# Who issues the loads of the key sums, and when the sums are made, in an attention kernel on one core

## The chip, the cores and the metric

One Trainium2 chip, one of its cores. The metric is the device time of one execution in microseconds. TensorE is called PE, VectorE DVE, ScalarE ACT, GpSimd POOL and SyncE SP in the profile.

## The reference

Cross attention with 16 heads of 64: 1024 queries, 6404 keys, model width 128, all float32, then a projection, a residual and a normalization.

```python
Q = (input_Q @ W_Q).reshape(b, -1, 16, 64).transpose(0, 2, 1, 3)      # x: (1, 1024, 128)
K = (input_K @ W_K).reshape(b, -1, 16, 64).transpose(0, 2, 1, 3)      # context: (1, 6404, 128)
V = (input_V @ W_V).reshape(b, -1, 16, 64).transpose(0, 2, 1, 3)
attn = softmax(einsum('bhqd,bhkd->bhqk', Q, K) / sqrt(64), axis=-1)
context = einsum('bhqk,bhkd->bhqd', attn, V).transpose(0, 2, 1, 3).reshape(b, -1, 1024)
out = context @ W_O + input_Q
return (out - mean(out)) / sqrt(var(out) + 1e-5)
```

## The kernel before

The heads go in eight pairs (0 to 7), and a pair in two halves of the queries (h = 0, 1), which makes 16 passes t. A pass runs over 50 chunks c of 128 keys; u counts the chunks of all passes. In step u PE computes the scores of chunk u + 2 (line 661) and adds the product of the probabilities and the values of chunk u (line 678). ACT makes the exponential of the scores (line 975, into a ring of four), DVE adds up the probabilities (line 1114). Each wait between engines is a semaphore; every engine runs its own list of instructions in the order in which it is written, and so does the DMA queue of the engine that issues a transfer.

Between the steps PE also computes the keys and values of the pair in blocks of four chunks; `work_at(t, c)` says which piece stands at which chunk. There are 12 full blocks and a rest. In pairs 1 to 7 the keys of the full blocks are computed by a Strassen-like scheme with seven products instead of eight. It needs sums of pieces of the context (the key sums, `c_forms`, here "forms", 384 KB per block) and of the weights. In a pass with h = 0 block b = c // 4 + 2 is served: at c % 4 = 0 the first round ("r", `seven_first`, lines 758 to 765), behind the product of its step, then three copies by ACT (`cross`, lines 991 and 993) and two sums by POOL (`sum_crossed`, lines 614 and 617); at c % 4 = 2 the second round ("k", `seven_second`, lines 776 to 780), which DVE takes out of PSUM (`take_seven`, lines 1095 to 1100); at c % 4 = 3 the values ("v", line 727), taken at line 1071. Blocks 0 and 1 of the next pair are served in the pass with h = 1, at chunks 38 to 45. The two rounds and the values share one pair of PSUM banks, so each waits until the one before is taken out.

The forms are the same for all pairs. POOL makes them once, in the first pass, from the context and a copy of it with its halves swapped (`form_keys`, four operations per block, lines 580 to 589, one after the other as their data comes). SP stores each block to DRAM (`store_forms`). From then on SP loads them, block by block and pair by pair, into the two places of `c_forms` (`load_forms`, line 460), 84 loads in all. A load waits for the second round that used the place before it, two blocks earlier. Where these loads stand among SP's other transfers is written out by hand in the loop of lines 478 to 510. That loop also carries the sums of the last pass: DVE folds them at chunk 8 of the next pass (line 1168), four small copies turn them (line 485), DVE inverts them at chunk 12 (lines 1176 to 1183), and they go through DRAM to all partitions (lines 491 to 501), for POOL's normalization at chunk 17. In a pass with h = 0 the loads of blocks 2 to 4 stand ahead of the wait for the fold, those of blocks 5 and 6 behind the four small copies, and the others behind the transfers of the inverses.

ACT issues two loads at the start (lines 995 and 996) and none after.

The loop of ACT, in short:

```python
for u in range(UNITS):
    t, c = place(u)
    if u + AHEAD < UNITS:
        exps(u + AHEAD)
    found = work_at(t, c)
    if found is not None and found[0] == "r":
        cross(found[1], found[2])
```

Of the kernel before, what the change touches and what calls it, by code (L numbers as in the profile page):

```python
# [6 lines left out]
ALU = mybir.AluOpType  # L7
# [4 lines left out]
def cross_attention_kernel(nc: bass.Bass, xT: bass.AP, x: bass.AP, ctxT: bass.AP, w_q: bass.AP,  # L12
# [27 lines left out]
    PAIRS = HD // (2 * DH)  # L40
    SCALE = float(DH) ** -0.5
    P = 128
# [19 lines left out]
    FULL_BLOCKS = NK // BK  # L62
# [18 lines left out]
    NORM_STEP, W_FORMS_STEP = 17, 24  # L81
    LAST_BLOCK_STEPS = (42, 45)
    LEFT_BEHIND = 7
    FORM_COLS = 2 * 3 * P
    assert NQH == 2 and BLOCKS == 13 and TAIL_CHUNKS == 3 and QT == 8
    assert CHUNKS == FULL_CHUNKS + 1 and LEFT_ROWS == DH

# [3 lines left out]
    def place(u):  # L91

        t = min(u // FULL_CHUNKS, PASSES - 1)
        return t, u - t * FULL_CHUNKS

    def by_seven(pair, b):

        return pair > 0 and 0 <= b < FULL_BLOCKS

    def seven_index(pair, b):  # L100
        return (pair - 1) * FULL_BLOCKS + b
# [34 lines left out]
    COUNT, READY = {}, {}  # L136
# [7 lines left out]
    with ctx:  # L144
# [53 lines left out]
        c_forms = sb("c_forms", [P, 2, FORM_COLS])  # L198
# [208 lines left out]
        def _(sp):  # L407
# [42 lines left out]
                sp.wait_ge(c_forms_ready, b + 1)  # L450
                sp.dma_start(forms_dram[b, :, :], c_forms[:, b % 2, :]).then_inc(c_forms_stored[b % 2], 16)

            def load_forms(pair, b):
                n = seven_index(pair, b)
                if n < 2:
                    for slot in range(2):
                        sp.wait_ge(c_forms_stored[slot], 16 * (FULL_BLOCKS // 2))
                else:
                    sp.wait_ge(work_done, COUNT["k", pair - (b < 2), (b - 2) % FULL_BLOCKS])
                sp.dma_start(c_forms[:, n % 2, :], forms_dram[b, :, :]).then_inc(c_forms_loaded[n % 2], 16)  # L460

            def load_turned_w(pair):
                if pair > 1:
# [13 lines left out]
            sp.wait_ge(left_zeroed, 2)  # L477
            for t in range(PASSES - 1):
                pair, h = (t + 1) // 2, (t + 1) % 2
                if h == 0:  # L480
                    for b in range(2, 5):
                        load_forms(pair, b)
                sp.wait_ge(quad_sums_ready, t + 1)
                for i in range(QUADS):
                    sp.dma_start(quad_rows[:, i, :], quad_sums[i * SQ:(i + 1) * SQ, :]).then_inc(quad_rows_loaded, 16)  # L485

                if h == 0:
                    for b in range(5, 7):
                        load_forms(pair, b)
                sp.wait_ge(inv_lines_ready, t + 1)  # L490
                sp.dma_start(inv_dram[t, :].rearrange("(j a) -> j a", a=SQ), inv_lines[:, :]).then_inc(inv_written, 16)
                sp.wait_ge(inv_written, 16 * (t + 1))
                if t > 0:
                    sp.wait_ge(norm_done, t)
                for head in range(2):
                    sp.dma_start(inv_sum[part(head), :], inv_dram[t, head * QH:(head + 1) * QH]
                                 .partition_broadcast(DH)).then_inc(inv_loaded, 16)
                for head in range(2):
                    row = t % 2 * DH + (t // 2 * 2 + head) * LEFT
                    sp.dma_start(inv_left[row:row + LEFT, :], inv_dram[t, head * QH:(head + 1) * QH]  # L500
                                 .partition_broadcast(LEFT)).then_inc(inv_left_loaded, 16)
                if t + 1 < PASSES - 1:
                    load_left(t + 1)
                if h == 1 and pair + 1 < PAIRS:
                    load_turned_w(pair + 1)
                    for b in range(2):
                        load_forms(pair + 1, b)
                if h == 0:
                    for b in range(7, FULL_BLOCKS):
                        load_forms(pair, b)  # L510

            def general():
                def load_weights(pair):
# [32 lines left out]
        def _(pool):  # L546
# [19 lines left out]
                nc.gpsimd.tensor_tensor(out=attn[:, pair, h * QH:(h + 1) * QH], in0=o_b[:, :], in1=inv_sum[:, :],  # L566
                                        op=ALU.mult).then_inc(norm_done, 1)

            def form_keys(b):

                one, two = part(b % 2), part(1 - b % 2)
                as_is = ctx_all[:, b * BK:(b + 1) * BK].rearrange("p (i e k) -> p i e k", i=2, e=2)
                turned = turned_ctx(b).rearrange("p (i e k) -> p i e k", i=2, e=2)
                forms = c_forms[:, b % 2, :].rearrange("p (i f k) -> p i f k", i=2, f=3)
                pool.wait_ge(ctx_loaded[b], 16)
                pool.wait_ge(chunk_loaded, 16)
                pool.wait_ge(turned_ctx_loaded[b % 2], 48 * (b // 2 + 1))
                if b > 0:
                    pool.wait_ge(c_forms_ready, b)
                nc.gpsimd.tensor_tensor(out=forms[one, :, 0:2, :], in0=as_is[one, :, :, :], in1=turned[one, :, :, :],  # L580
                                        op=ALU.add).then_inc(c_form_step, 1)
                pool.wait_ge(c_form_step, 3 * b + 1)
                nc.gpsimd.tensor_tensor(out=forms[two, :, 0, :], in0=as_is[two, :, 1, :], in1=turned[two, :, 0, :],
                                        op=ALU.subtract).then_inc(c_form_step, 1)
                pool.wait_ge(c_form_step, 3 * b + 2)
                nc.gpsimd.tensor_tensor(out=forms[two, :, 1, :], in0=as_is[two, :, 0, :], in1=as_is[two, :, 1, :],
                                        op=ALU.add).then_inc(c_form_step, 1)
                pool.wait_ge(c_form_step, 3 * b + 3)
                nc.gpsimd.tensor_tensor(out=forms[two, :, 2, :], in0=turned[two, :, 0, :], in1=turned[two, :, 1, :],
                                        op=ALU.add).then_inc(c_forms_ready, 1)  # L590

            def form_weights(pair):

# [25 lines left out]

            pool.wait_ge(identity_ready, 2)  # L620
            pool.wait_ge(left_zeroed, 2)
            for b in range(FULL_BLOCKS):
                form_keys(b)
            pool.wait_ge(c_forms_ready, FULL_BLOCKS)
            for t in range(1, PASSES):
                for c in range(FULL_CHUNKS):
# [341 lines left out]
        def _(act):  # L968
# [14 lines left out]
            def cross(pair, b):  # L983
# [8 lines left out]
                                         ACT.Copy).then_inc(crossed_ready, 1)  # L992
                nc.scalar.activation(crossed[:, 0, :], seven_slots(b)[2], ACT.Copy).then_inc(crossed_ready, 1)  # L993

            act.dma_start(wq_sb[:, 0:2 * DH], w_q[:, 0:2 * DH]).then_inc(first_w_loaded["q"], 16)
            act.dma_start(xT_sb[:, 0:QH], xT[:, 0:QH]).then_inc(x_loaded[0], 16)
            for found in WHOLE:
# [3 lines left out]
# [4 lines that stand above are left out]
                found = work_at(t, c)  # L1005
                if found is not None and found[0] == "r":
                    cross(found[1], found[2])
                if t == 0 and c == LEFT_EXP_STEP:

                    act.wait_ge(work_ready, READY["sl", 0, 0])  # L1010
                    nc.scalar.activation(p_left[:, :], p_left[:, :], ACT.Exp, scale=SCALE).then_inc(left_ready, 1)
                if c == chunks_of(t) - 1:

                    act.wait_ge(pv_done, u + 1)
                    if t > 0:

                        act.wait_ge(norm_done, t)
                    nc.scalar.activation(o_a[:, :], o_ps[:, 0, :], ACT.Copy).then_inc(o_a_ready, 1)  # L1018
# [359 lines left out]
```

## Time and profile before

| | |
|---|---|
| median of 3 runs | 1603.39 us (1603.27 to 1603.54) |
| profiled execution | 1603.11 us, span 1601.3 us |
| granted clock of TensorE, mean | 0.999 |
| PE busy | 1586.4 us, 99% |
| DVE, ACT, POOL busy | 84%, 58%, 18% |
| DMA, mean over the span | 35 GB/s |

The busy time of PE contains modelled ends: a matmul counts as busy until its modelled end, also when the next one has already started. Idle time of PE in the profile is therefore what is left after these ends; the distance between the starts of two groups shows more.

### The profile page before, as it was taken

Reading aid. Unit: us, or ns where it says so; the run is one execution under the profiler, and the core shown is the slowest. Engines: PE = TensorE matmul, PEld = TensorE weight load, DVE = VectorE, ACT = ScalarE, POOL = GpSimd, SP = SyncE. Lnnn points to the kernel's source line nnn. Section 1 sums busy time; section 2 is a strip of 40 time slices with the busy share of each in tenths; the row PEclk is TensorE's granted clock in tenths of the full one; section 3 lists DMA queues with packets and bytes.
Section 4 is the critical chain, followed back from the end, with each engine's and each line's share of the span. In section 5 each row is a group of like instructions: output and inputs, shape, how many; then the busy total and the mean of one; then the engine's idle time right before and its main releaser. Section 6 shows DMA issues by size and latency. Waiting matters only on the chain.

```text
span 1601.3 us, 43898 instructions
## 1 busy us (share of the span) xinstructions
PE 1586.4 (99%) x19164; PEld 1028.4 (64%) x19164; DVE 1346.4 (84%) x1397; ACT 929.7 (58%) x1080; POOL 294.5 (18%) x313
## 2 busy tenths in 40 slices
PE   9999999999999999999999999999999999999998
PEld 4576666666666666666666666666666666666435
DVE  7898798887988878887798878888788887898877
ACT  4345566556555556656566566565666555656653
POOL 4842012120121201202022021120111102111000
PEclk9999999999999999999999999999999999999999
DMA  6320002010110001100011000110011100110000
GB/s 214 94 76 31 11 22 69 12 31 11 42 58 2 30 22 39 51 2 31 21 49 41 2 31 21 59 32 2 30 32 49 32 2 30 32 59 22 9 1 15
DMA packets 31618, 56.68 MB, mean 35 GB/s; under 512 B 7120, under 2 KB 13392, under 8 KB 31424
## 3 DMA queue, kind: packets, MB, share of 16 engines
q1 hardware_dynamic: 31136, 53.51, 10.6%
q8 instruction: 153, 2.51, 0.7%
q14 instruction: 41, 0.34, 0.1%
q10 hardware_dynamic: 288, 0.33, 0.1%
HBM read 48.02 MB, written 5.30 MB: 33 GB/s over the span
## 4 chain that ended last, share of the span: by engine, by line
PE 93%; DVE 3%; DMA 2%; issue 1%; SPq 1%; ACT 0%; DVEq 0%; ACTq 0%
PE s_ps L661 41%; PE o_ps L678 41%; PE w_ps L727 5%; PE w_ps L744 2%; DMA c_forms<-forms_dram 2%; DVE sums L1114 1%; SPq L485 1%; PE w_ps L758 1%; PE w_ps L763 1%; PE w_ps L780 1%; DVE quad_sums L1168 1%; PE w_ps L779 1%; PE w_ps L759 0%; PE w_ps L776 0%; PE w_ps L765 0%
## 5 line engine op out<-in xcount | busy, mean ns | idle before, releaser
L975 ACT ACTIVATE probs<-s_ps 128x1024 f32<-128x1024 f32 x801 | 820.6, 1025 | 619.2 <-PE s_ps L661 611.7
L1114 DVE TENSOR_TENSOR sums<-sums,probs 128x1024 f32<-128x1024 f32 x785 | 986.3, 1256 | 123.1 <-ACT probs L975 89.8
L678 PE MATMUL o_ps<-probs,v_all 64*64 64x512 f32 x6408 | 927.2, 589 | 0.0
L661 PE MATMUL s_ps<-q_sb,k_all 64*64 64x512 f32 x6408 | 924.7, 589 | 0.0
L678 PEld LDWEIGHTS o_ps<-probs,v_all 64*64 64x64 f32 x6408 | 412.4, 133 | 219.1 <-issue 89.3
L661 PEld LDWEIGHTS s_ps<-q_sb,k_all 64*64 64x64 f32 x6408 | 401.2, 133 | 202.0 <-issue 76.7
L614 POOL TENSOR_TENSOR crossed<-crossed 128x128 f32<-128x128 f32 x84 | 43.6, 519 | 721.3 <-ACT crossed L993 721.3
L1071 DVE TENSOR_REDUCE v_all<-w_ps 128x512 f32<-128x1024 f32 (+2 forms) x103 | 122.0, 1184 | 41.8 <-PE w_ps L727 41.6
L727 PEld LDWEIGHTS w_ps<-wv_sb,ctx_all 64*64 64x64 f32 x3176 | 110.4, 133 | 42.6 <-issue 16.6
L727 PE MATMUL w_ps<-wv_sb,ctx_all 64*64 64x128 f32 x3176 | 117.3, 269 | 0.0
L991 ACT ACTIVATE crossed<-w_ps 64x384 f32<-64x384 f32 x168 | 81.6, 486 | 24.2 <-PE w_ps L765 22.0
L617 POOL TENSOR_TENSOR crossed<-crossed 128x128 f32<-128x128 f32 x84 | 90.6, 1078 | 6.6
L560 POOL TENSOR_TENSOR o_b<-o_a,o_b 128x512 f32<-128x512 f32 x15 | 23.5, 1565 | 248.8 <-ACT o_a L1018 248.8
L1095 DVE TENSOR_TENSOR k_all<-crossed,w_ps 128x256 f32<-128x256 f32 x84 | 35.3, 420 | 37.3 <-POOL crossed L617 27.2
L566 POOL TENSOR_TENSOR attn<-o_b,inv_sum 128x512 f32<-128x512 f32 x15 | 25.8, 1718 | 210.9 <-DMA inv_sum<-inv_dram 210.9
L780 PEld LDWEIGHTS w_ps<-ctx_all,w_forms 64*64 64x64 f32 x336 | 41.3, 133 | 25.9 <-issue 18.5
L1097 DVE TENSOR_REDUCE k_all<-w_ps 128x256 f32<-128x512 f32 x84 | 57.4, 683 | 0.0
L758 PEld LDWEIGHTS w_ps<-c_forms,w_forms 64*64 64x64 f32 x336 | 21.2, 131 | 49.0 <-DVE v_all L1071 39.4
L780 PE MATMUL w_ps<-ctx_all,w_forms 64*64 64x128 f32 x336 | 51.3, 269 | 0.0
L779 PE MATMUL w_ps<-c_forms,w_forms 64*64 64x128 f32 x336 | 48.9, 269 | 0.0
L779 PEld LDWEIGHTS w_ps<-c_forms,w_forms 64*64 64x64 f32 x336 | 39.3, 133 | 4.3 <-issue 3.2
L758 PE MATMUL w_ps<-c_forms,w_forms 64*64 64x128 f32 x336 | 34.6, 274 | 5.8 <-DMA c_forms<-forms_dram 5.8
(115 smaller groups left out, 686.1 us busy)
## 6 DMA issues: line engine op xcount, KB each, us to landing
c_forms<-forms_dram SPq DMA_DIRECT2D x84, 384.0 KB, 3.1
forms_dram<-c_forms SPq DMA_DIRECT2D x12, 384.0 KB, 2.6
inv_sum<-inv_dram SPq DMA_DIRECT2D x30, 128.0 KB, 2.8
attn<-in_ctxT SPq DMA_DIRECT2D x24, 128.0 KB, 3.3
ctx_all<-in_ctxT SPq DMA_DIRECT2D x11, 256.0 KB, 5.3
quad_rows<-quad_sums SPq DMA_DIRECT2D x60, 4.0 KB, 1.8
c_forms<-in_ctxT SPq DMA_DIRECT2D x12, 64.0 KB, 2.4
x_sb<-in_x SPq DMA_DIRECT2D x1, 512.0 KB, 10.1
```

The lines of the kernel that those rows point to most:

```text
L617: nc.gpsimd.tensor_tensor(out=crossed[:, 0, :], in0=crossed[:, m3, :], in1=crossed[:, m1, :], op=ALU.subtract).then_inc(crossed_summed, 1)
L661: last = nc.tensor.matmul(s_ps[part(half), u % 2, head * QH:(head + 1) * QH], k_all[part(head), c * P + half * DH:c * P + (half + 1) * DH] ...
L678: last = nc.tensor.matmul(o_ps[part(head), rows, :], v_all[part(rows), key_chunk(t, c, head), part(head)], probs[part(rows), u % RING, hea ...
L727: last = nc.tensor.matmul(banks[rows][part(half), m * P:(m + 1) * P], ctx_all[part(rows), at_key:at_key + DH], wv_sb[part(rows), at * P:(a ...
L758: nc.tensor.matmul(main[g, 0, 1, :], w_form(one, 0, 1 - i), form(one, pair, b, i, 0), start=True, stop=True)
L779: nc.tensor.matmul(main[part(i), 1, 0, :], w_form(one, 1, i), form(one, pair, b, i, 2), start=True, stop=True)
L780: last = nc.tensor.matmul(main[part(1 - i), 0, 0, :], w_form(one, 2, 1 - i), ctx_all[part(one), at:at + P], start=True, stop=True)
L975: nc.scalar.activation(probs[:, u % RING, :], s_ps[:, u % 2, :], ACT.Exp, scale=SCALE).then_inc(probs_ready, 1)
L991: nc.scalar.activation(crossed[part(1 - half), 1:4, :], apart[part(half), :, :], ACT.Copy).then_inc(crossed_ready, 1)
L1071: return nc.vector.tensor_reduce(out=target, in_=banks.rearrange("p r n -> p n r"), axis=AX.X, op=ALU.add)
L1097: nc.vector.tensor_reduce(out=target[:, :, 1, :], in_=main.rearrange("p j s k -> p j k s"), axis=AX.X, op=ALU.add)
L1114: nc.vector.tensor_tensor(out=sums[0:rows, t % 2, :], in0=sums[0:rows, t % 2, :], in1=probs[0:rows, u % RING, :], op=ALU.add).then_inc(sum ...
```

## The change

The loads of the forms leave SP's list, but for the first two (pair 1, blocks 0 and 1). ACT gets them: in its loop, in the step after a second round, and behind the exponential of that step, it waits for that second round and issues the load of the block two further on, which may belong to the next pair. POOL makes the forms in steps: operation number n of the 48 (n = 0 to 47) waits, beside what it waited for, until exponential number n is done. Nothing that is computed changes.

```diff
--- before.py
+++ after.py
@@ -81,7 +81,7 @@
     NORM_STEP, W_FORMS_STEP = 17, 24
     LAST_BLOCK_STEPS = (42, 45)
     LEFT_BEHIND = 7
-    FORM_COLS = 2 * 3 * P
+    FORM_COLS, FORM_STEPS = 2 * 3 * P, 4
     assert NQH == 2 and BLOCKS == 13 and TAIL_CHUNKS == 3 and QT == 8
     assert CHUNKS == FULL_CHUNKS + 1 and LEFT_ROWS == DH
 
@@ -450,14 +450,11 @@
                 sp.wait_ge(c_forms_ready, b + 1)
                 sp.dma_start(forms_dram[b, :, :], c_forms[:, b % 2, :]).then_inc(c_forms_stored[b % 2], 16)
 
-            def load_forms(pair, b):
-                n = seven_index(pair, b)
-                if n < 2:
-                    for slot in range(2):
-                        sp.wait_ge(c_forms_stored[slot], 16 * (FULL_BLOCKS // 2))
-                else:
-                    sp.wait_ge(work_done, COUNT["k", pair - (b < 2), (b - 2) % FULL_BLOCKS])
-                sp.dma_start(c_forms[:, n % 2, :], forms_dram[b, :, :]).then_inc(c_forms_loaded[n % 2], 16)
+            def load_first_forms():
+                for slot in range(2):
+                    sp.wait_ge(c_forms_stored[slot], 16 * (FULL_BLOCKS // 2))
+                for b in range(2):
+                    sp.dma_start(c_forms[:, b, :], forms_dram[b, :, :]).then_inc(c_forms_loaded[b], 16)
 
             def load_turned_w(pair):
                 if pair > 1:
@@ -477,16 +474,10 @@
             sp.wait_ge(left_zeroed, 2)
             for t in range(PASSES - 1):
                 pair, h = (t + 1) // 2, (t + 1) % 2
-                if h == 0:
-                    for b in range(2, 5):
-                        load_forms(pair, b)
                 sp.wait_ge(quad_sums_ready, t + 1)
                 for i in range(QUADS):
                     sp.dma_start(quad_rows[:, i, :], quad_sums[i * SQ:(i + 1) * SQ, :]).then_inc(quad_rows_loaded, 16)
 
-                if h == 0:
-                    for b in range(5, 7):
-                        load_forms(pair, b)
                 sp.wait_ge(inv_lines_ready, t + 1)
                 sp.dma_start(inv_dram[t, :].rearrange("(j a) -> j a", a=SQ), inv_lines[:, :]).then_inc(inv_written, 16)
                 sp.wait_ge(inv_written, 16 * (t + 1))
@@ -503,11 +494,8 @@
                     load_left(t + 1)
                 if h == 1 and pair + 1 < PAIRS:
                     load_turned_w(pair + 1)
-                    for b in range(2):
-                        load_forms(pair + 1, b)
-                if h == 0:
-                    for b in range(7, FULL_BLOCKS):
-                        load_forms(pair, b)
+                    if pair == 0:
+                        load_first_forms()
 
             def general():
                 def load_weights(pair):
@@ -566,28 +554,31 @@
                 nc.gpsimd.tensor_tensor(out=attn[:, pair, h * QH:(h + 1) * QH], in0=o_b[:, :], in1=inv_sum[:, :],
                                         op=ALU.mult).then_inc(norm_done, 1)
 
-            def form_keys(b):
+            def form_keys(b, step):
 
                 one, two = part(b % 2), part(1 - b % 2)
                 as_is = ctx_all[:, b * BK:(b + 1) * BK].rearrange("p (i e k) -> p i e k", i=2, e=2)
                 turned = turned_ctx(b).rearrange("p (i e k) -> p i e k", i=2, e=2)
                 forms = c_forms[:, b % 2, :].rearrange("p (i f k) -> p i f k", i=2, f=3)
-                pool.wait_ge(ctx_loaded[b], 16)
-                pool.wait_ge(chunk_loaded, 16)
-                pool.wait_ge(turned_ctx_loaded[b % 2], 48 * (b // 2 + 1))
-                if b > 0:
-                    pool.wait_ge(c_forms_ready, b)
-                nc.gpsimd.tensor_tensor(out=forms[one, :, 0:2, :], in0=as_is[one, :, :, :], in1=turned[one, :, :, :],
-                                        op=ALU.add).then_inc(c_form_step, 1)
-                pool.wait_ge(c_form_step, 3 * b + 1)
-                nc.gpsimd.tensor_tensor(out=forms[two, :, 0, :], in0=as_is[two, :, 1, :], in1=turned[two, :, 0, :],
-                                        op=ALU.subtract).then_inc(c_form_step, 1)
-                pool.wait_ge(c_form_step, 3 * b + 2)
-                nc.gpsimd.tensor_tensor(out=forms[two, :, 1, :], in0=as_is[two, :, 0, :], in1=as_is[two, :, 1, :],
-                                        op=ALU.add).then_inc(c_form_step, 1)
-                pool.wait_ge(c_form_step, 3 * b + 3)
-                nc.gpsimd.tensor_tensor(out=forms[two, :, 2, :], in0=turned[two, :, 0, :], in1=turned[two, :, 1, :],
-                                        op=ALU.add).then_inc(c_forms_ready, 1)
+                if step == 0:
+                    pool.wait_ge(ctx_loaded[b], 16)
+                    pool.wait_ge(chunk_loaded, 16)
+                    pool.wait_ge(turned_ctx_loaded[b % 2], 48 * (b // 2 + 1))
+                    if b > 0:
+                        pool.wait_ge(c_forms_ready, b)
+                    nc.gpsimd.tensor_tensor(out=forms[one, :, 0:2, :], in0=as_is[one, :, :, :],
+                                            in1=turned[one, :, :, :], op=ALU.add).then_inc(c_form_step, 1)
+                    return
+                pool.wait_ge(c_form_step, 3 * b + step)
+                if step == 1:
+                    nc.gpsimd.tensor_tensor(out=forms[two, :, 0, :], in0=as_is[two, :, 1, :], in1=turned[two, :, 0, :],
+                                            op=ALU.subtract).then_inc(c_form_step, 1)
+                elif step == 2:
+                    nc.gpsimd.tensor_tensor(out=forms[two, :, 1, :], in0=as_is[two, :, 0, :], in1=as_is[two, :, 1, :],
+                                            op=ALU.add).then_inc(c_form_step, 1)
+                else:
+                    nc.gpsimd.tensor_tensor(out=forms[two, :, 2, :], in0=turned[two, :, 0, :], in1=turned[two, :, 1, :],
+                                            op=ALU.add).then_inc(c_forms_ready, 1)
 
             def form_weights(pair):
 
@@ -619,8 +610,9 @@
 
             pool.wait_ge(identity_ready, 2)
             pool.wait_ge(left_zeroed, 2)
-            for b in range(FULL_BLOCKS):
-                form_keys(b)
+            for c in range(FORM_STEPS * FULL_BLOCKS):
+                pool.wait_ge(probs_ready, c + 1)
+                form_keys(c // FORM_STEPS, c % FORM_STEPS)
             pool.wait_ge(c_forms_ready, FULL_BLOCKS)
             for t in range(1, PASSES):
                 for c in range(FULL_CHUNKS):
@@ -992,6 +984,14 @@
                                          ACT.Copy).then_inc(crossed_ready, 1)
                 nc.scalar.activation(crossed[:, 0, :], seven_slots(b)[2], ACT.Copy).then_inc(crossed_ready, 1)
 
+            def load_forms(behind):
+
+                _, pair, b = behind
+                n = seven_index(pair, b) + 2
+                if n < (PAIRS - 1) * FULL_BLOCKS:
+                    act.wait_ge(work_done, COUNT[behind])
+                    act.dma_start(c_forms[:, n % 2, :], forms_dram[n % FULL_BLOCKS, :, :]).then_inc(c_forms_loaded[n % 2], 16)
+
             act.dma_start(wq_sb[:, 0:2 * DH], w_q[:, 0:2 * DH]).then_inc(first_w_loaded["q"], 16)
             act.dma_start(xT_sb[:, 0:QH], xT[:, 0:QH]).then_inc(x_loaded[0], 16)
             for found in WHOLE:
@@ -1005,6 +1005,9 @@
                 found = work_at(t, c)
                 if found is not None and found[0] == "r":
                     cross(found[1], found[2])
+                done = work_at(*place(u - 1)) if u > 0 else None
+                if done is not None and done[0] == "k" and by_seven(done[1], done[2]):
+                    load_forms(done)
                 if t == 0 and c == LEFT_EXP_STEP:
 
                     act.wait_ge(work_ready, READY["sl", 0, 0])
```

## Rows read from the trace of the kernel before

**Rows 1.** The page, busy time of each engine, share of the span, instructions.

```profile
PE 1586.4 (99%) x19164; PEld 1028.4 (64%) x19164; DVE 1346.4 (84%) x1397; ACT 929.7 (58%) x1080; POOL 294.5 (18%) x313
```

**Rows 2.** The page, chain that ended last, by engine.

```profile
PE 93%; DVE 3%; DMA 2%; issue 1%; SPq 1%; ACT 0%; DVEq 0%; ACTq 0%
```

**Rows 3.** Waits of all engines: total us, times, longest us.

```profile
PE w_ps L758 <- DMA c_forms<-forms_dram: 5.8, 7, 1.8
...
PE w_ps L796 <- DVE k_all L1071: 0.7, 1, 0.7
```

**Rows 4.** Waits of SP's DMA queue, the same columns.

```profile
SPq L485 <- DVE quad_sums L1168: 503.7, 14, 55.5
```

**Rows 5.** Timeline of PE: start, us, instruction, idle before and its releaser.

```profile
240.40 1.08 PE L661 MATMUL s_ps<-q_sb,k_all 64*64 64x512 f32 x8
241.26 1.08 PE L678 MATMUL o_ps<-probs,v_all 64*64 64x512 f32 x8
242.90 0.29 PE L758 MATMUL w_ps<-c_forms,w_forms 64*64 64x128 f32 x1 [0.56 <-DMA c_forms<-forms_dram]
...
1219.94 0.29 PE L758 MATMUL w_ps<-c_forms,w_forms 64*64 64x128 f32 x1 [1.83 <-DMA c_forms<-forms_dram]
...
1414.98 0.29 PE L758 MATMUL w_ps<-c_forms,w_forms 64*64 64x128 f32 x1 [0.43 <-DMA c_forms<-forms_dram]
```

**Rows 6.** Timeline of SP's DMA queue, first place of Rows 5.

```profile
237.05 2.46 SPq L485 DMA_DIRECT2D quad_rows<-quad_sums  x4
239.55 1.06 SPq L460 DMA_DIRECT2D c_forms<-forms_dram  x2
```

**Rows 7.** Line 460: ns min/median/max of the issue, and to landing.

```profile
L460 SPq DMA_DIRECT2D c_forms<-forms_dram x84: 319/331/736, 154.1 to 1452.7; - x84
...
DMA to landing us min/median/max: 2.8/3.1/5.3
```

**Rows 8.** Timeline of ScalarE, 224 to 262 us, between two key blocks.

```profile
230.57 1.02 ACT L975 ACTIVATE probs<-s_ps 128x1024 f32<-128x1024 f32 x1 [1.09 <-PE s_ps L661]
233.16 1.03 ACT L975 ACTIVATE probs<-s_ps 128x1024 f32<-128x1024 f32 x1 [1.56 <-PE s_ps L661]
234.37 0.99 ACT L991 ACTIVATE crossed<-w_ps 64x384 f32<-64x384 f32 x2 [0.19 <-PE w_ps L765]
```

**Rows 9.** Timeline of ScalarE's DMA queue at the start.

```profile
1.18 0.45 ACTq L996 DMA_DIRECT2D xT_sb<-in_xT  x1
```

**Rows 10.** Timeline of GpSimd, key sums in the first pass.

```profile
24.41 1.62 POOL L580 TENSOR_TENSOR c_forms<-ctx_all,attn 64x512 f32<-64x512 f32 x1 [21.72 <-DMA c_forms<-in_ctxT]
...
58.50 0.72 POOL L589 TENSOR_TENSOR c_forms<-attn 64x256 f32<-64x256 f32 x1
...
104.40 1.59 POOL L589 TENSOR_TENSOR c_forms<-attn 64x256 f32<-64x256 f32 x1
```

**Rows 11.** Timeline of ScalarE in the first pass, the 24th exponential.

```profile
62.05 1.02 ACT L975 ACTIVATE probs<-s_ps 128x1024 f32<-128x1024 f32 x1 [1.64 <-PE s_ps L661]
```

**Rows 12.** VectorE's sums by line, first 24 to 107 us, then 107 to 190.

```profile
L1114 DVE TENSOR_TENSOR sums<-sums,probs 128x1024 f32<-128x1024 f32 x35 | 52.1, 1489 | 1.2
...
L1114 DVE TENSOR_TENSOR sums<-sums,probs 128x1024 f32<-128x1024 f32 x47 | 58.6, 1248 | 12.4 <-ACT probs L975 10.8
```

**Rows 13.** Timeline of PE, value work of the step after the first place.

```profile
248.76 1.15 PE L727 MATMUL w_ps<-wv_sb,ctx_all 64*64 64x128 f32 x30
```

**Rows 14.** Timeline of VectorE, 122 to 127 us and 224 to 272 us.

```profile
124.10 0.69 DVE L1198 COPY o_b<-o_ps 128x512 f32<-128x512 f32 x1 [1.92 <-PE o_ps L678]
...
240.71 1.23 DVE L1071 TENSOR_REDUCE v_all<-w_ps 128x512 f32<-128x1024 f32 x1 [0.16 <-PE w_ps L727]
...
245.37 1.20 DVE L1114 TENSOR_TENSOR sums<-sums,probs 128x1024 f32<-128x1024 f32 x1
247.00 0.42 DVE L1095 TENSOR_TENSOR k_all<-crossed,w_ps 128x256 f32<-128x256 f32 x1 [0.43 <-POOL crossed L617]
...
247.94 0.41 DVE L1100 TENSOR_TENSOR k_all<-k_all,w_ps 128x256 f32<-128x256 f32 x1
```

## The prediction

> **What bounds the kernel now.** I read the busy times first. The reader is to see one engine, PE, at 99% and the next, VectorE, at 84% [rows 1]: whatever the others do counts only where it makes PE late. The chain that ended last says the same, with 93% on PE, but it also gives 2% to a DMA and 1% to SP's queue [rows 2], which no engine-bound kernel would show. So the third view is the waits. Of all waits put down to PE's matmuls after the start only two kinds are left: line 758, the first round of a key block, on the load of its key sums, 7 times, 5.8 us in all and at most 1.8, and line 796, once, on VectorE, 0.7 us [rows 3]. Seven is the number of pairs that work with these sums (1 to 7), so it is one place in each pair.
>
> The fourth view is the timeline at these places. Matmul ends are modelled, so I go by starts: the groups of eight matmuls start 0.86 us apart (240.40, 241.26), so the array could have taken the next work at 242.12, and it starts at 242.90 [rows 5]. That is 0.78 us, where the profile says 0.56 idle, 0.22 more. The last view is SP's queue there [rows 6]. The load that PE waits for (block 5 of the pair, first round at chunk 12) goes out at 239.55, straight behind the four small copies of the row sums, which themselves could not start until VectorE's fold at chunk 8 was done; SP spends 503.7 us of the run in that wait [rows 4]. The buffer that the load fills had been free since the second round of block 3, at chunk 6. It is a load held up by its place in SP's program and by nothing else.
>
> **The change, part by part.** (1) The loads leave SP. 84 stand there now, 2 stay (pair 1, blocks 0 and 1, issued at the same point as before), 82 go to ScalarE. What is lost of PE's time goes with them: 5.8 us of waits and 7 x 0.22 of what the modelled ends hide, 7.3 us. From both sides: not under 5.8, and were the hidden part as long as 0.3 at each place, 7.9. I take 7.3, by the place that I read.
>
> Does the load come early enough from ScalarE? It is issued one step after the second round whose sums it overwrites, behind that step's exponential. For block 5 that is the exponential of 230.57, over at 231.59 [rows 8]; with 0.45 us for the issue and even the longest landing of the trace, 5.3 [rows 7], the sums are there at 237.3, 4.8 us before 242.12. All other blocks have the same distance of two blocks, eight chunks at 1.7 us or more each, so no load is late. ScalarE's wait on the second round never holds it: that work stands on PE before the scores which the exponential ahead of the wait has already read.
>
> (2) What the issues cost ScalarE. Behind the waiting load stand the next exponential, then the three copies of the first round, and PE waits for both. The load's slot is the gap after the exponential of the step with value work, and there ScalarE sits idle 1.56 us before the next exponential at 233.16 [rows 8]. Nothing in the trace shows this load issued by ScalarE; its own first issues are near: 0.45 us [rows 9], and SP's for this very load 0.32 to 0.74 [rows 7]. Between 0.32 and 0.74 I take 0.45. All of it lies in the 1.56: cost 0. ScalarE's next idle time is 0.19 before the copies [rows 8], so cover ends at 1.75 us per issue; only beyond that do copies and then PE move.
>
> (3) What SP gains. 82 issues of 0.33 are gone from a queue that is mostly waiting. The copies of the sums and of the inverses go out at the same point or earlier; GpSimd's and VectorE's use of them is not on PE's path. 0. The load for block 6 now leaves ScalarE half a microsecond from where SP issued it, 0 too.
>
> (4) The key sums in the first pass. Same 48 operations on GpSimd, but each waits for one more exponential. They begin at 24.41, when their data has landed [rows 10], and by then some eight exponentials are done, so the first half runs back to back as now. The 24th sum starts at 58.50 now [rows 10] and the 24th exponential ends at 63.07 [rows 11]: from about there on the sums are paced, one per chunk. The last now starts at 104.40 [rows 10]; it will start a chunk or two before the pass ends, near 118, still ahead of GpSimd's next task (the add after the copy at 124.10) and of the first loads. What lies beside it is VectorE: its sums take 1489 ns on average while GpSimd works and 1248 after [rows 12], so 35 x 0.24 = 8.4 us are lost there today. That loss is nearly all hidden, as PE shows a single stall in the pass (0.7 us at line 796 [rows 3]), early, while the sums still run back to back in both kernels. Spread out, the conflict reaches chunks 44 to 47, where it did not. There VectorE would be later by some 5 x 0.24 = 1.2 us, and it idles 1.92 before the copy that ends the pass [rows 14]. Bounds: from -0.9 (the one stall goes) to +8.4 (the whole conflict comes out on PE). I take 0, as the same conflict cost PE almost nothing where it was densest.
>
> (5) What is late next, at the seven places. VectorE takes no breath there: it was not waiting for the load, so it keeps its clock while PE moves 0.78 earlier. Value work just before is taken by 241.94 (240.71 + 1.23) [rows 14], under 242.12, so the first round can start. After it, VectorE's sum at 245.37 ends at 246.57 and its key work begins 0.43 later [rows 14]; so key work can move up by 0.43. It ends at 248.35 now, and becomes 247.92. The value work on PE that waits for it is at 248.76 [rows 13] and would be at 247.98. It fits by 0.06 us. Cost 0, but this is the thinnest cover in the sum.
>
> Sum: -7.3 + 0 + 0 + 0 + 0. The profiled execution took 1603.11 us (span 1601.3 and 1.8 around it), 0.28 under the median of 1603.39; 1603.11 - 7.3 = 1595.8, and against the median 1596.1.
>
> **A rule weighed.** Block 5's load is ready to go eight microseconds before SP gets to it [rows 6, 8]. The Trainium skill, "DMA: Bandwidth & Descriptors", section "Issuing engines are not separate DMA queues", says that DMAs started by different engines share the same 16 DMA engines and that issuing from several saves only the issue time. Read by itself it would leave nothing of the 7.3 us but two issues' time; that is rival 2, and the trace speaks against it here, since what was long was the wait ahead of the issue.
>
> **Rivals.** (1) VectorE takes the load's place. For: the cover of 0.06 us in (5), and a fold and an inversion of about a microsecond each that stand close together there. Against: the key work that ends at 248.35 today leaves 0.41 us before 248.76, and with its own 0.43 that is more than the 0.78 asked. If only VectorE's own slack of 0.43 per place can be had, the gain is 7 x 0.43 = 3.0: 1600.4. (2) The issue's place was not the cause: the transfer itself, or something it shares, keeps the sums late, and nothing is gained. For: landing times spread from 2.8 to 5.3 [rows 7], and the longest stall (2.05 by starts) is far from the shortest. Against: 4.8 us of reserve. 1603.4. This is also the case that the change doesn't do what it says. (3) The other side: a DMA issue holds ScalarE. The point from which it decides is 1.75 us. If ScalarE were held until the data lands, 3.1 in the median [rows 7], each of the 82 would push copies and key work back by 3.1 - 1.75 = 1.35, 111 us, less 7.3: about 1707. Against: its first issue took 0.45 [rows 9]. (4) The first pass gets worse: all 8.4 us of conflict shown, with the gain kept: 1604.5. Against: see (4) of the parts.
>
> **How the numbers follow.** Forecast 0.76; rival 1, 0.08; rival 2, 0.05; rival 3, 0.03; rival 4 in full, 0.02; and 0.06 for partial forms of 1 and 4 that end between 1597 and 1600.2. A measurement of this kernel can tell about 0.2%, 3.2 us, from no change. Faster by more than that: the forecast and the partial forms, 0.82. Within it: rivals 1, 2 and 4, and a little of 3 in a mild form, 0.14. Slower: 0.04. The range runs from the upper bound of the gain with the one stall gone, 1603.4 - 7.9 - 0.9 = 1594.6, to rival 1, 1600.4. The predicted time is 1596.1.
>
> **What would show each step.** Right: in the waits no line 758 on a load, and its issues under ScalarE's queue, 82, of 0.3 to 0.8 us, with the exponentials still waiting for PE behind them; PE's starts 0.86 apart through chunk 12 of each pair. The 24th key sum and later ones start just behind their exponential, and the last near 118 us. The forecast is wrong if line 758 or 727 now waits for VectorE at chunks 12 to 16, if PE shows new stalls in the first 125 us, or if the exponentials after an issue wait for nothing that PE does.

## The result, and the profile after

The changed kernel took 1595.41 us in the median of 6 runs (1594.34 to 1595.74), the kernel before 1603.33 us in six runs beside and before it (1602.12 to 1603.74). The ratio is 0.9950, 95% interval 0.9938 to 0.9963. The forecast was 1596.1 in 1594.6 to 1600.4. The profiled execution took 1595.61 us with a span of 1593.7, 7.5 and 7.6 less than before.

From the page of the kernel after: busy time by engine, and the chain that ended last. They answer to [rows 1, 2].

```profile
PE 1584.4 (99%) x19164; PEld 986.4 (62%) x19164; DVE 1344.2 (84%) x1397; ACT 929.0 (58%) x1080; POOL 286.3 (18%) x313
...
PE 97%; DVE 2%; issue 1%; ACT 0%; DVEq 0%; ACTq 0%
```

The work is the same and PE's share is still 99%; what changed is that DMA and SP's queue are gone from the chain. Before, they held 3% of it. That share is not the gain (it counts the whole way back from a stall); the gain is 0.5%.

The timeline of PE at the first of the seven places, after (start, us, instruction, idle before). It answers to [rows 5].

```profile
240.52 1.09 PE L653 MATMUL s_ps<-q_sb,k_all 64*64 64x512 f32 x8
241.37 1.09 PE L670 MATMUL o_ps<-probs,v_all 64*64 64x512 f32 x8
242.23 0.28 PE L750 MATMUL w_ps<-c_forms,w_forms 64*64 64x128 f32 x2
```

The first round now starts 0.86 after the product, one group's pace. Before, it was 1.64. Read so at all seven places, the first round before stood 1.51 to 2.91 behind the product, together 7.5 us over seven times 0.86. After, all seven are at 0.86. In the waits of this kernel no matmul waits for `c_forms` any more. SP simply sleeps longer ahead of the same four copies, as its waits show (total us, times, longest us; [rows 4] had 503.7).

```profile
SPq L479 <- DVE quad_sums L1171: 1177.5, 14, 85.5
```

The loads under their new queue, line 993 (ns min/median/max of the issue, then issue to landing), the answer to [rows 7]:

```profile
L993 ACTq DMA_DIRECT2D c_forms<-forms_dram x82: 326/326/352, 198.1 to 1446.7; - x82
...
DMA to landing us min/median/max: 2.7/3.1/5.5
```

And ScalarE's timeline at the step of [rows 8]:

```profile
230.68 1.02 ACT L967 ACTIVATE probs<-s_ps 128x1024 f32<-128x1024 f32 x1 [1.09 <-PE s_ps L653]
230.71 0.33 ACTq L993 DMA_DIRECT2D c_forms<-forms_dram  x1
233.27 1.02 ACT L967 ACTIVATE probs<-s_ps 128x1024 f32<-128x1024 f32 x1 [1.57 <-PE s_ps L653]
```

The exponential behind the issue still waits for PE, as long as before (1.57 against 1.56). One thing here I had not foreseen: the load stands behind the exponential in ScalarE's program, but it goes out at 230.71, 0.03 us after that exponential has started, not at its end at 231.70.

The first pass: GpSimd's 24th and last key sum, VectorE's sums in the two stretches of [rows 12], and VectorE's copy and key work of [rows 14].

```profile
63.40 1.71 POOL L580 TENSOR_TENSOR c_forms<-attn 64x256 f32<-64x256 f32 x1 [2.40 <-ACT probs L967]
...
117.67 0.96 POOL L580 TENSOR_TENSOR c_forms<-attn 64x256 f32<-64x256 f32 x1 [0.77 <-ACT probs L967]
```

```profile
L1117 DVE TENSOR_TENSOR sums<-sums,probs 128x1024 f32<-128x1024 f32 x35 | 49.3, 1408 | 1.2
...
L1117 DVE TENSOR_TENSOR sums<-sums,probs 128x1024 f32<-128x1024 f32 x46 | 58.6, 1274 | 12.3 <-ACT probs L967 10.8
```

```profile
124.21 0.69 DVE L1201 COPY o_b<-o_ps 128x512 f32<-128x512 f32 x1 [0.50 <-PE o_ps L670]
...
246.62 0.40 DVE L1098 TENSOR_TENSOR k_all<-crossed,w_ps 128x256 f32<-128x256 f32 x1
...
247.55 0.40 DVE L1103 TENSOR_TENSOR k_all<-k_all,w_ps 128x256 f32<-128x256 f32 x1
```

The sums are paced and spread: VectorE loses 81 ns less per sum up to 107 us (1489 to 1408) and 26 more after (1248 to 1274), and its idle time ahead of the copy that ends the pass shrank from 1.92 to 0.50. PE shows none of this at the end of the pass. Its starts give two short stalls, 0.45 us at the left-over keys (0.89 before) and 0.51 at the values of the step at 59 us, which is new. Together that is 0.96 us for the 0.89 before.

### The profile page after: what moved, and what is told of

It reads as the page before. It is cut to its first block, busy times and chain, and to the rows that moved or that the text cites. A ratio compares the mean times of both kernels' runs of the same rounds, so it can differ in the third digit from the quotient of the medians.

```text
span 1593.7 us, 43934 instructions
## 1 busy us (share of the span) xinstructions
PE 1584.4 (99%) x19164; PEld 986.4 (62%) x19164; DVE 1344.2 (84%) x1397; ACT 929.0 (58%) x1080; POOL 286.3 (18%) x313
## 4 chain that ended last, share of the span: by engine, by line
PE 97%; DVE 2%; issue 1%; ACT 0%; DVEq 0%; ACTq 0%
PE s_ps L653 43%; PE o_ps L670 43%; PE w_ps L719 5%; PE w_ps L736 2%; DVE sums L1117 1%; PE w_ps L750 1%; PE w_ps L755 1%; PE w_ps L771 1%; PE w_ps L772 1%; PE w_ps L751 1%; PE w_ps L768 1%; PE w_ps L757 0%; PE s_ps L848 0%; DVE inv_sum L1227 0%; DVE y L1260 0%
## 5 line engine op out<-in xcount | busy, mean ns | idle before, releaser
L670 PEld LDWEIGHTS o_ps<-probs,v_all 64*64 64x64 f32 x6408 | 390.4, 133 | 240.0 <-issue 115.6
L653 PEld LDWEIGHTS s_ps<-q_sb,k_all 64*64 64x64 f32 x6408 | 382.6, 133 | 219.3 <-issue 100.3
L605 POOL TENSOR_TENSOR crossed<-crossed 128x128 f32<-128x128 f32 x84 | 41.8, 498 | 717.7 <-ACT crossed L985 717.7
L608 POOL TENSOR_TENSOR crossed<-crossed 128x128 f32<-128x128 f32 x84 | 86.7, 1032 | 6.6
L771 PE MATMUL w_ps<-c_forms,w_forms 64*64 64x128 f32 x336 | 50.4, 269 | 0.0
L1103 DVE TENSOR_TENSOR k_all<-k_all,w_ps 128x256 f32<-128x256 f32 x84 | 34.4, 409 | 0.0
```

The source lines that it names most:

```text
L605: nc.gpsimd.tensor_tensor(out=crossed[:, m4, :], in0=crossed[:, m4, :], in1=crossed[:, 0, :], op=ALU.subtract).then_inc(crossed_summed, 1)
L608: nc.gpsimd.tensor_tensor(out=crossed[:, 0, :], in0=crossed[:, m3, :], in1=crossed[:, m1, :], op=ALU.subtract).then_inc(crossed_summed, 1)
L653: last = nc.tensor.matmul(s_ps[part(half), u % 2, head * QH:(head + 1) * QH], k_all[part(head), c * P + half * DH:c * P + (half + 1) * DH] ...
L670: last = nc.tensor.matmul(o_ps[part(head), rows, :], v_all[part(rows), key_chunk(t, c, head), part(head)], probs[part(rows), u % RING, hea ...
L771: nc.tensor.matmul(main[part(i), 1, 0, :], w_form(one, 1, i), form(one, pair, b, i, 2), start=True, stop=True)
```

## The experiments

**Each half alone.** Theory A: the whole gain is the seven stalls, and they come from where the loads stand in SP's list. Theory B: the spread sums give a part. The first kernel moves the loads and leaves the sums back to back (`form_keys` is again that of the kernel before):

```diff
-            for c in range(FORM_STEPS * FULL_BLOCKS):
-                pool.wait_ge(probs_ready, c + 1)
-                form_keys(c // FORM_STEPS, c % FORM_STEPS)
+            for b in range(FULL_BLOCKS):
+                form_keys(b)
```

> The loads of the key sums go to ScalarE as in the change, but GpSimd makes the sums back to back as before. Theory A (the whole gain is the seven stalls at chunk 12 of pairs 1 to 7, caused by the loads' place in SP's list): ratio to before 0.9952 to 0.9956, about 1596 us; no wait of line 750 on a load; the stall in the first pass at line 788 as before, 0.9 us by starts. Theory B (a part of the gain comes from the spread sums in the first pass, where VectorE's sums fell from 1489 to 1408 ns on average between 24 and 107 us, 2.8 us in all): 2 to 3 us less gain, about 1598.5.

Measured: 1595.85 us (5 runs), ratio 0.9949, interval 0.9935 to 0.9963. No matmul waits for a load. The stall at the left-over keys was 0.36, less than the 0.9 I expected from the same back-to-back sums; why it differs is not shown. The loads alone give the gain of the whole change, and B's 1598.5 is outside.

The second kernel is the other half: the sums paced as in the change, the 84 loads in SP's list as before.

> GpSimd makes the sums one step per chunk, the loads stay in SP's list as before. Theory A: no gain, 1603.4, ratio 0.9995 to 1.0005; seven stalls on the loads, 5 to 6 us idle; in the first pass one stall a little shorter and one new one of half a microsecond. Theory B: 1600.5, ratio 0.998. Also tested: whether VectorE's later copy at the end of the first pass (idle before it 0.50 instead of 1.92) costs PE anything; A says nothing.

Measured: 1602.80 us (11 runs), ratio 1.0000, interval 0.9991 to 1.0009. The seven waits are there, in the waits of that kernel:

```profile
PE w_ps L762 <- DMA c_forms<-forms_dram: 5.9, 7, 1.9
```

The pacing is worth nothing that can be measured (the interval is 1.5 us to either side), and so the late copy at the end of the first pass costs nothing that can be measured either.

**The place in the list, with SP still issuing.** The kernel before with one number changed in two lines. Block 5's load moves ahead of SP's wait for the fold:

```diff
                 if h == 0:
-                    for b in range(2, 5):
+                    for b in range(2, 6):
                         load_forms(pair, b)
                 sp.wait_ge(quad_sums_ready, t + 1)
...
                 if h == 0:
-                    for b in range(5, 7):
+                    for b in range(6, 7):
                         load_forms(pair, b)
```

> The kernel before with one load moved in SP's own list: the load of block 5 stands ahead of SP's wait for the fold of the row sums, with those of blocks 2 to 4, and not behind the four small copies. No load goes to ScalarE. Theory A (the place in the list, not the engine that issues): the seven stalls go, 1596, ratio 0.9952 to 0.9956, as in the change. Theory C (what helps is another queue, or SP having less to issue): the stalls stay, 1603.4. If block 6's load, which stays behind the copies, comes late in its turn, a wait of line 758 shows at chunk 16 instead; A expects none, since it is issued at 240 and needed at 251.

Measured: 1596.06 us (5 runs), ratio 0.9950, interval 0.9937 to 0.9964. The waits on loads are gone from PE, at chunk 12 and at chunk 16. So all of the change's gain can be had by moving seven of the 84 issues within SP's own list. ScalarE's queue as such adds nothing that can be measured. The Trainium skill ("DMA: Bandwidth & Descriptors", "Issuing engines are not separate DMA queues") says that DMAs share the same 16 DMA engines whichever engine starts them, and that issuing from several engines saves only the time of the issue. This case agrees: the landing is 3.1 us in the median under both queues. Issue time was not what the old place cost either: the load had stood behind a wait on another engine.

**How much the head start was.** If a load is late only when it lands after the moment at which PE could start the first round (its need), delaying all of them must cost nothing up to a point and then cost at nearly every block. Two kernels, after the change, with the load four and five steps behind the second round in place of one:

```diff
-                done = work_at(*place(u - 1)) if u > 0 else None
+                done = work_at(*place(u - 4)) if u > 3 else None
```

The second has `u - 5` and `u > 4`.

> The kernel after the change with each load on ScalarE three steps later (four behind the second round). For block 5 that is behind the exponential that starts at 237.14, so the sums land at about 240.3 in the median and PE wants them at 242.23. Theory A: only landings over 5.1 us are late, the longest in the trace was 5.5: 1595.4 to 1596.5, at most a few short waits of line 750. If what counts is not the single load but how many transfers are under way at once (rival 2 of the prediction in another form), the landings change and it is over 1600.

Measured: 1595.03 us (4 runs), ratio 0.9946, interval 0.9929 to 0.9963; no matmul waits for a load.

> The kernel after the change with each load on ScalarE four steps later, five steps behind the second round whose place it fills. For block 5 that is behind the exponential that starts at 239.18 in the trace, so the sums land at about 239.2 + 3.1 = 242.3 in the median, and PE wants them at 242.23. Theory A (a load is late exactly by issue plus landing less need): most of the 82 places stall by 0.1 to 0.5 us and a few by up to 2.5, together 8 to 40 us over 1595.4, waits of line 750 on the loads at nearly all blocks. If PE's need were later than I read from the starts, or the landing shorter, 1595.4.

Measured: 1625.22 us (4 runs), ratio 1.0134, interval 1.0119 to 1.0150, 29.8 over the change. The waits of that kernel:

```profile
PE w_ps L750 <- DMA c_forms<-forms_dram: 16.3, 20, 2.0
```

One step more turns 0 into 30 us, inside the 8 to 40 forecast. The row gives only 16.3 of the 30 us, but PE's starts give all of it: over all first rounds, the distance from the product beyond 0.86 us adds up to 37.2 us here and to 6.8 in the kernel after the change. Where a stall is short, the modelled ends cover it.

The landings show the rule at each load. In this kernel 54 of the 84 first rounds start 0.14 us after their load has landed, and so do the seven late ones of the kernel before. These loads are the eight of each pair behind the first four, 56 in all, of which two just missed being late; the 30 us are some 0.5 us for each. The other loads have 4 us or more in hand. The place for which I had worked out the times is one of the two:

```profile
238.98 0.33 ACTq L993 DMA_DIRECT2D c_forms<-forms_dram  x1
...
241.92 0.30 PE L750 MATMUL w_ps<-c_forms,w_forms 64*64 64x128 f32 x2
```

The load goes out at 238.98 and lands after 2.71 us, at 241.69, less than the 3.1 of the median; the first round starts on time. With three steps more the least time between a landing and its first round is 1.4 us, and in the kernel after the change it is 6.0.

**What an issue may cost ScalarE.** Cover is the time that the issues may take before the copies behind them move. Theory P is the forecast's: the issue starts when the exponential ahead is over, cover 1.75 us. Theory O came with the trace after: it starts beside that exponential, cover 1.02 + 1.57 + 0.19 = 2.8 us from the exponential's start. Behind each load ScalarE issues k more small loads, into a tile that nobody reads (the tile, its semaphore and the wait for the last of them are left out here):

```diff
                     act.dma_start(c_forms[:, n % 2, :], forms_dram[n % FULL_BLOCKS, :, :]).then_inc(c_forms_loaded[n % 2], 16)
+                    if n > 2:
+                        act.wait_ge(spare_loaded, 16 * k * (n - 2))
+                    for i in range(k):
+                        act.dma_start(spare[:, i, :], ctxT[:, i * 4:i * 4 + 4]).then_inc(spare_loaded, 16)
```

> The kernel after the change; behind each load ScalarE issues two more small ones (128 rows of 16 bytes into a tile that nobody reads), 82 x 3 issues of about 0.33 us, 1.0 us per place. Theory P (as predicted: an issue starts when the exponential ahead of it is over, and the cover is 1.56 + 0.19 = 1.75 us): no cost, 1595.4. Theory O (as the trace after suggests: an issue starts 0.03 us after the start of the exponential ahead of it, beside it, so the cover is 1.02 more, 2.8 us): no cost either. A cost here would say that each issue holds more than it shows.

Measured: 1595.50 us (4 runs), ratio 0.9950, interval 0.9933 to 0.9967: nothing.

> The same with six more small loads, seven issues, 7 x 0.33 = 2.3 us per place. Theory P (cover 1.75): copies and key work late by 0.55 at 82 places, of which PE has some 0.1 to 0.4 in hand: 10 to 45 us more, 1605 to 1640. Theory O (cover 2.8): no cost, 1595.4 to 1596.5, with the exponential behind the issues still waiting for PE.

Measured: 1629.63 us (4 runs), ratio 1.0163, interval 1.0146 to 1.0180: 34 more. At first sight that is P's range. But that range was worked out from a wrong issue time. ScalarE's timeline of this kernel:

```profile
222.24 1.03 ACT L969 ACTIVATE probs<-s_ps 128x1024 f32<-128x1024 f32 x1 [1.13 <-PE s_ps L655]
222.26 0.33 ACTq L995 DMA_DIRECT2D c_forms<-forms_dram  x1
222.64 3.79 ACTq L999 DMA_DIRECT2D spare<-in_ctxT  x6
226.55 1.02 ACT L969 ACTIVATE probs<-s_ps 128x1024 f32<-128x1024 f32 x1 [3.29 <-DMA spare<-in_ctxT]
```

A small issue takes 0.45 us in the median, not 0.33, and some take up to 2.43 (line 999 of that kernel). Here seven issues held the queue from 222.26 to 226.43, 4.2 us where I had put 2.3; over the 82 places it is 3.3 in the median and 3.7 in the mean. The exponential behind them does not wait for the small loads to land, whatever the row's releaser says: the one wait on small loads stands ahead of the issues and is for those of the place before, and the exponential starts 0.12 us behind the last issue in the median. The time is over the cover of either theory. An estimate from the times of the 82 places, with 0.1 to 0.4 us that PE has in hand at each, gives 125 to 150 us under P and 41 to 66 under O. The measured 34 is below both, but only P is far off.

> The same with ten more, eleven issues, 3.6 us per place. Theory P: late by 1.9 us per place, about 130 us more. Theory O: late by 0.8 less what PE has in hand (0.1 to 0.4), 82 places: 30 to 65 us more, 1625 to 1660.

Measured: 1836.89 us (4 runs), ratio 1.1461, interval 1.1442 to 1.1480, 241 more, far over both ranges, for the same reason. Eleven issues hold the queue 6.4 us at the place that I read (226.00 to 232.35), 6.0 in the median. A part of the 241 is the clock, whose mean grant fell to 0.974: in 27 stretches of 3.4 us, 92 us in all, it was granted at half, 1.2 GHz, which can have cost 46 us at most. The same estimate gives 302 to 327 us under P and 218 to 242 under O, both without the clock, so P is too dear here too.

With the issue time as measured, a kernel with four more small loads was to decide:

> The kernel after the change with four more small loads behind each load on ScalarE. In the run with six more, a small issue took 0.45 us in the median, so five issues hold the queue 0.38 + 4 x 0.48 = 2.3 us from the start of the first. Theory P (an issue starts when the exponential ahead of it is over; cover 1.75 us): late by 0.55 at 82 places, 12 to 37 us more, 1607 to 1632. Theory O (it starts beside that exponential; cover 2.8 us from the exponential's start): no cost but for a few long issues, 1595.4 to 1598.

Measured: 1597.81 us (4 runs), ratio 0.9958, interval 0.9943 to 0.9974. The kernel before took 1604.22 beside it, so by ratios this is 1.3 us over the change, within the two intervals. ScalarE's timeline:

```profile
221.69 1.02 ACT L969 ACTIVATE probs<-s_ps 128x1024 f32<-128x1024 f32 x1 [0.95 <-PE s_ps L655]
221.71 0.33 ACTq L995 DMA_DIRECT2D c_forms<-forms_dram  x1
222.09 1.89 ACTq L999 DMA_DIRECT2D spare<-in_ctxT  x4
224.28 1.02 ACT L969 ACTIVATE probs<-s_ps 128x1024 f32<-128x1024 f32 x1 [1.57 <-PE s_ps L655]
```

Five issues end at 223.98, and the next exponential starts at 224.28, after 1.57 idle, still on PE's word. Had they begun at the exponential's end at 222.71, they would have ended at 224.98 and delayed it by 0.7. Five issues take 2.3 us in the median, and at 11 of the 82 places more than 2.8. Theory O holds, P is out (it wanted 12 us at least).

**GpSimd's conflict with VectorE in the first pass.** The forecast took it as hidden. In this kernel each key sum is made twice; the first of the four operations is shown, the others are changed alike:

```diff
+                    nc.gpsimd.tensor_tensor(out=forms[one, :, 0:2, :], in0=as_is[one, :, :, :],
+                                            in1=turned[one, :, :, :], op=ALU.add).then_inc(form_twice, 1)
+                    pool.wait_ge(form_twice, 4 * b + 1)
                     nc.gpsimd.tensor_tensor(out=forms[one, :, 0:2, :], in0=as_is[one, :, :, :],
...
```

> The kernel after the change with each of the 48 key sums made twice on GpSimd (the second time with the same result), so GpSimd is busy nearly the whole first pass. Theory A (the conflict with VectorE in the first pass is nearly all hidden, and the cover is thin): VectorE's sums go from about 1408 to 1550 to 1650 ns on average between 24 and 107 us, 35 x 0.2 = 7 us more for VectorE, of which 1 to 6 us come out as stalls of PE at lines 719, 788 and at the end of the pass: 1596.5 to 1601.5. If the conflict had wide cover, 1595.4. If GpSimd falls behind the chunks, its last sum ends after 124 us and delays the add of the halves, which has cover up to chunk 4 of the next pass.

Measured: 1617.15 us (5 runs), ratio 1.0078, interval 1.0064 to 1.0092, some 21 over the change and far over the range. VectorE's sums averaged 1619 ns between 24 and 107 us, as expected. But the price came from elsewhere. VectorE's timeline:

```profile
114.16 1.33 DVE L1137 TENSOR_TENSOR sums<-sums,left_rows 4x1024 f32<-4x1024 f32 x1 [4.79 <-DMA left_rows<-p_left]
...
171.62 0.35 DVE L1192 TENSOR_REDUCE inv_rows<-quad_rows 32x32 f32<-32x128 f32 x1 [14.66 <-DMA quad_rows<-quad_sums]
```

and SP's queue at the second place:

```profile
159.26 8.08 SPq L452 DMA_DIRECT2D forms_dram<-c_forms  x2
167.45 2.97 SPq L480 DMA_DIRECT2D quad_rows<-quad_sums  x4
```

GpSimd ran until 167 us. SP waits for it block by block before it stores the sums, and the copies that VectorE needs stand behind these stores. VectorE stood still for 14.66 us, and PE's starts show a gap of 14.0 at 161, and 4.3 at 113 from the first place; those two are 18.3 of the 21. The clock is about the rest. Behind each gap it was granted at half, 1.2 GHz, until 120.9 and until 178.9 us; PE worked 3.1 and 3.9 us at that level, and half of these 7.0 us is lost. The conflict itself shows in PE as little more than the 0.7 at the left-over keys. So "the conflict is hidden" survives. What I had missed is that a late GpSimd reaches PE through SP's list. The order in the traces shows this; no run moved the stores.

## Why the prediction was right

**The seven stalls, -7.3.** They are gone, and the loads alone give the gain (ratio 0.9949). The term was sized by one place (0.22 us beside what the idle column says) times seven. PE's starts at all seven give 7.5 us, so 0.25 each, and the profiled executions differ by 7.5. The medians differ by 7.9; the 0.4 between is less than the spread of the runs. The step that carries it, that the load was held up by its place in SP's list, was shown by the kernel that moved it there: 1596.06.

**Early enough from ScalarE.** Right, with more in hand than I gave it: the load leaves 0.9 us sooner. The limit was tested from the late side: 0 at three steps more and 30 us at four.

**Issues on ScalarE, 0.** Right in size, at 0.33 us an issue (I took 0.45). Wrong in the mechanism, and the cover of 1.75 us was too small by the exponential's 1.02: five issues in 2.3 us cost 1.3 us in all by the ratios, no clear difference from nothing.

**SP's part, 0.** Right. Only the load of block 6 moved by more than the half microsecond said, from 240.18 to 239.20, and nothing waited for it.

**The key sums in the first pass, 0.** Right: pacing alone has a ratio of 1.0000. The last sum was forecast near 118 and started at 117.67; VectorE's loss at the end was put at 1.2 us and was 1.42. The bounds of -0.9 and +8.4 treated only the direct conflict. The path through SP's list, seen in the last experiment, was in none of my rivals; the traces leave it harmless in the changed kernel, where GpSimd's last sum starts at 117.67, and costly where GpSimd lags: at 113 us, ahead of the left-over rows, and at 161, ahead of the fold's copies.

**What is late next, 0.** Right, and by as little as said: VectorE's key work was forecast to start at 246.57 and end at 247.92; it starts at 246.62 and ends at 247.95. The value work on PE behind it, forecast at 247.98, starts at 248.10, one group's pace behind the product, so no new stall came.

**The rivals.** VectorE in the load's place: excluded by the result. The place not being the cause: excluded by the moved load within SP. ScalarE held: its point of decision exists, but lies at 2.8 us after the exponential's start, and an issue takes an eighth of that. The first pass getting worse: excluded by the pacing alone. One slip stands in the chances: rivals 1, 2 and 4 add up to 0.15, where 0.14 is given to an outcome within the noise; the forecast does not hang on it.

## What to carry to other kernels

When a load is late, first look at what stands ahead of its issue in its queue's program. If that is a wait on another engine, try to move the load ahead of the wait: here that was worth as much as moving it to another engine, and is the smaller edit. Then work out its slack, the time of PE's need less that of the issue and the landing: here some 2 us of slack cost nothing and none cost 30 us. Where the idle column hides short stalls, the distance between starts finds them. And a queue whose stores wait for one engine ties everything behind them to that engine.

## What the runs showed of the hardware that was not expected

A DMA issue that stands behind an exponential on ScalarE goes out 0.03 us after that exponential starts, beside it (230.68 and 230.71; 0.03 is also the median of the 82 places). Its own wait was met by then. The issue of a load of 128 rows of 3072 bytes took 0.33 us and that of 128 rows of 16 bytes 0.45: the smaller one is the longer. In rows of six, single issues took up to 2.43 us; why is open. In the kernels with six and ten small loads the next exponential starts 0.12 us behind the last issue in the median, so issues that go out beside one exponential hold the next. Where PE waited for a load, its first matmul started 0.14 us after the landing, at all seven places before the change and at 54 in the kernel with four steps more.
